# A Mamba block and a table-coded FFN on one core: the time steps move in the merged stages, three pieces of work move in the prologue

## The chip, the cores and the metric

One core of a Trainium2 chip runs the whole kernel in one launch. The time is the device time of that core in microseconds (us). The engines, by the names of the profile: PE is TensorE, DVE is VectorE, ACT is ScalarE, POOL is GpSimd, SP is SyncE, which here only issues DMAs. Each engine works through its own queue in order; they wait for each other on semaphores.

## The reference

For an input of 4 x 1024 tokens of 512 numbers:

```python
x = x + layernorm(mamba(layernorm(x)))          # mamba: below
x = x + layernorm(ffn(layernorm(x)))
# mamba(u): proj = u @ W_in.T, split into z (512), x (512), B (64), C (64), dt (8 heads)
#   x, B, C = silu(causal_conv4(x, B, C));  dt = softplus(dt + dt_bias);  dA = exp(-exp(A_log) * dt)
#   S = S * dA_t + dt_t * outer(x_t, B_t);  y_t = S @ C_t          (a scan over the tokens of a sequence)
#   y = (y + D * x) * silu(z);  return y @ W_out.T
# ffn(x): w = lut[idx] for the three matrices (16 values), h = silu(x @ gate.T) * (x @ up.T), h @ down.T
```

`W_in` is 1160 x 512, the FFN's inner width is 1376. State and `dt` are per head (8 heads of 64).

## The kernel before

**Tiles and stages.** The 4096 tokens are cut into 8 tiles of 512 tokens (t = 0 to 7), each of 4 chunks of 128. Every fp32 operand of a large product is split into two fp16 halves, so that a product is three matmuls. After a prologue the kernel runs 8 stages and two tails. Stage t does the scan of tile t chunk by chunk (four phases: `scan(t, c)` on PE, `y_sum`, `y_gated`, `y_split` on DVE, `segments`, `weights`, `decay_state` on POOL) and prepares tile t+1: its projections, the causal convolution of five blocks of 128 channels (`conv`, order 4, 0, 1, 2, 3, block 4 being B and C), the gates `z`, and the time steps. In stages 0 and 1 (`dec`) the FFN's weights are decoded beside this: ACT turns codes into fp16 (`codes_to_half`), DVE makes eight masks for each unit of 832 columns (`masks`), PE multiplies them with a diagonal of the table's values (`decode`), ACT copies the result (`decoded`). In stages 2 to 7 (`ffn`, "merged stages") the FFN of tile g = t - 2 runs beside the scan: `gate_up(g, m)` for 11 blocks m, then `down(g, c)` for 4 chunks. The two tails are the FFN of tiles 6 and 7.

**What sets the order.** Every engine's order of work is written out by hand in its own `stage(t)` function (POOL L670, ACT L910, PE L1346, DVE L1694, SP's L465 and L509), and its prologue ahead of them. Nothing is planned at run time: an instruction whose input is late holds up all behind it on its engine.

**PE and its banks.** `gate_up(g, m)` (L1312) writes gate m, then up m, into three PSUM banks in turn. Turn n needs the bank of turn n - 3 read: gate m is read by `gate_silu(g, m)`, up m by `times_up(g, m)`, both DVE, and both count on the semaphore `ffn_turn`. So up 7 (turn 15) needs `gate_silu(6)` and what stands before it in DVE's queue, gate 8 needs `times_up(6)`, up 8 needs `gate_silu(7)`, up 9 needs `gate_silu(8)`. In the second phase of a merged stage PE does: scan 1, projections of dt and conv 4, gate/up 5, `prepare` and segment sums of chunk 2, gate/up 6, conv 0, gate/up 7, `project_out` 1, gate/up 8; then scan 2, conv 1, gate/up 9.

**DVE's second phase** in `stage` (L1745 to L1791): y of chunk 1, `dt_input(t+1)`, `conv(t+1, 4)`, `gate_silu(5)`, `times_up(5)`, `weigh`, `decayed`, `conv_silu(t+1, 4)`, `time_steps(t+1)`, `ln_stats("x", t-1, 0)`, `gate_silu(6)`, `low(5)`, `times_up(6)`, `conv(t+1, 0)`, `gate_silu(7)`, `low(6)`, `conv_silu(t+1, 0)`, `times_up(7)`, `gate_silu(8)`, `low(7)`, `times_up(8)`; then `y_sum(t, 2)`.
`time_steps(i)` (L1562) is a chain of 18 instructions on 128 x 32 numbers: the softplus's series, `da` in two fp16 halves (step 20 of `dt_steps`), and `dt4` (step 21). Its readers are `segments(t+1, 0)` on POOL (L597), which waits for step 20, PE's `prepare_small(t+1, 0)` and POOL's `weights(t+1, 0)`, all in the fourth phase. `ln_stats` (L1517) takes mean and variance of a pair of slices (two `bn_stats`, two `bn_aggr`); POOL's `pair_rstd` (L585, five small operations) makes the scale and shift of them; ACT's `normalise_slice` (L775) applies them. POOL's `pair_rstd("x", t-1, 0)` stands between `weights(t, 2)` and `decay_state(t, 2)`.

**The prologue.** Input slices 0 are normalised, transposed and projected; `W_in` is scaled and split on ACT and DVE (`high_half`, `low_half`); the same is done for `W_out`, whose scale (`scales(1)` and `c_out`) DVE makes after a maximum over partitions on POOL (L758). ACT's `high_half(3)` (L1132) waits for it on `s_wscale`, and DVE's `out_weights_low` in stage 0 needs that. DVE's order from L1974: `dt_input(0)`, out scale, `conv(0, 0)`, `conv_silu(0, 4)`, `conv_silu(0, 0)`, `time_steps(0)`, `conv(0, 1)`, `ln_stats("u", 1, 0)`, `z_gate(0, 0)`, `conv(0, 2)`, `conv_silu(0, 1)`, `conv(0, 3)`, `conv_silu(0, 2)`, `clear_state(0)`, `z_gate(0, 1)`, `conv_silu(0, 3)`, `weigh(0, 0)`, `decayed(0, 0)` (the first decayed gram), `z_gate(0, 2)`, `masks(0)`, `z_gate(0, 3)`. On POOL, `pair_rstd("u", 1, 0)` (L764) stands ahead of `segments(0, 0)` and `weights(0, 0)`. On ACT `codes_to_half(3)` (L1151) waits until all of `masks(0)` is made.

Of the kernel before, what the change touches and what calls it, by code (L numbers as in the profile page):

```python
# [120 lines left out]
def sandwich_kernel(nc, u, w_in_t, conv_w, conv_b, w_out_t, a_log, d_param, dt_bias, lut, codes, out):  # L121
# [31 lines left out]
    with ctx:  # L153
# [242 lines left out]
        with nc.Block() as block:  # L396
# [184 lines left out]
            def _(pool):  # L581
# [3 lines left out]
                def pair_rstd(kind, tile, b):  # L585
                    no = pair_no[kind, tile, b]
                    i = no % 2
                    v = vare[:, i, :]
                    pool.wait_ge(ln_steps.sem, ln_steps.now(no, 4))
                    for n, (dst, a, b, op) in enumerate((  # L590
                            (v, mv[:, i, :, 1], eps_c[:, 0:2], ALU.add), (v, v, neg_half[:, 0:2], ALU.pow),
                            (rstd[:, i, :], v, xs_c[:, 0:2], ALU.mult), (v, mv[:, i, :, 0], neg_one[:, 0:2], ALU.mult),
                            (shift[:, i, :], v, rstd[:, i, :], ALU.mult))):
                        rstd_steps.inc(nc.gpsimd.tensor_tensor(dst, a, b, op))  # L594
                        pool.wait_ge(rstd_steps.sem, rstd_steps.now(no, n + 1))

                def segments(t, c):  # L597
                    if t > 0 or c > 0:
                        pool.wait_ge(y_done.sem, y_done.now(t, c))
                    if c == 0:  # L600
                        pool.wait_ge(dt_steps.sem, dt_steps.now(t, 20))
                    for n in range(2):
                        seg_ready.inc(nc.gpsimd.tensor_tensor(  # L603
                            segs[:, n], causal_h[:].unsqueeze(1).broadcast_to((P, HEADS, P)),
                            da[:, t % HALVES, c, n, :].unsqueeze(2).broadcast_to((P, HEADS, P)), ALU.mult))
# [64 lines left out]
                def stage(t):  # L670
                    g = t - LAG
                    nxt = t + 1 < TILES

                    decay_state(t, 0)
                    segments(t, 1)
                    if t >= 1:
                        out_rstd(t - 1, 3)
                        add_residual(t - 1, 3)
                    weights(t, 1)
                    if nxt:  # L680
                        pair_rstd("u", t + 1, 1)

                    decay_state(t, 1)
                    segments(t, 2)
                    out_rstd(t, 0)
                    add_residual(t, 0)
                    weights(t, 2)
                    if t >= 1:
                        pair_rstd("x", t - 1, 0)

                    decay_state(t, 2)
                    segments(t, 3)
                    out_rstd(t, 1)
                    add_residual(t, 1)
                    weights(t, 3)

                    decay_state(t, 3)
                    if nxt:
                        segments(t + 1, 0)
                    if g >= 0:  # L700
                        down_rstd(g, 0)
                    out_rstd(t, 2)
                    if g >= 0:
                        add_output(g, 0)
                    add_residual(t, 2)
                    if g >= 0:
                        down_rstd(g, 1)
                    if nxt:
                        weights(t + 1, 0)
                    if t >= 1:  # L710
                        pair_rstd("x", t - 1, 1)
                    if g >= 0:
                        add_output(g, 1)
                        down_rstd(g, 2)
                        add_output(g, 2)
                    if t + 2 < TILES:
                        pair_rstd("u", t + 2, 0)
                    if g >= 0:
                        down_rstd(g, 3)
                        add_output(g, 3)  # L720

                def tail(t):
# [38 lines left out]
                    diag[:], fold[:].unsqueeze(1).unsqueeze(1).broadcast_to((P, PAIRS, 2, NST)),  # L761
                    lut_sel[:].rearrange("p n q -> p q n").unsqueeze(3).broadcast_to((P, PAIRS, 2, NST)),
                    ALU.mult).then_inc(s_diag, 1)
                pair_rstd("u", 1, 0)  # L764
                segments(0, 0)
                weights(0, 0)
                for t in range(TILES):
# [5 lines left out]
            def _(act):  # L773
# [71 lines left out]
                def codes_to_half(k):  # L845

                    if k >= HALF_UNITS:
                        return
                    act.wait_ge(s_codes[k % 2], 32 * (k // 2 + 1))
                    if k >= CODE_SLOTS:  # L850
                        act.wait_ge(s_masks, 2 * (k - CODE_SLOTS + 1))
                    nc.scalar.activation(codes_h[:, k % CODE_SLOTS, :], codes_sb[:, k % 2, :], ACT.Identity,
                                         bias=pair_bias[:]).then_inc(s_half, 1)
# [248 lines left out]
                def high_half(n):  # L1102
                    src, hi, _, which = PIECES[n]
                    act.wait_ge(s_wscale if which else s_scale, 1)
                    nc.scalar.activation(hi, src, ACT.Copy, scale=wscale[:, which:which + 1]).then_inc(s_whi if which else s_hi, 1)
# [23 lines left out]
                conv_input(0, 0)  # L1129
                dt_exponential(0)  # L1130
                conv_tanh(0, 4)
                high_half(3)  # L1132
                conv_tanh(0, 0)
                conv_input(0, 1)
                act.wait_ge(s_pair, 1)
# [12 lines left out]
                codes_to_half(1)  # L1148
                z_tanh(0, 3)
                codes_to_half(2)  # L1150
                codes_to_half(3)  # L1151
                for t in range(TILES):
                    stage(t)
# [334 lines left out]
            def _(dve):  # L1488
# [51 lines left out]
                def conv_silu(i, f):  # L1540
                    o = CONV_ORDER.index(f)
                    half = i % HALVES
                    dve.wait_ge(ctanh_ready.sem, ctanh_ready.now(i, o + 1))
                    if f < KC:
                        xs_ready.inc(nc.vector.scalar_tensor_tensor(
                            xs[:, half, f, :], conv_in(i, o)[:, 0:TILE], 1.0, xs[:, half, f, :], ALU.add, ALU.mult))
                    else:
                        h = slice(half * NST, (half + 1) * NST)
                        for dst, lo in ((bs, 0), (cs, NST)):
                            xs_ready.inc(nc.vector.scalar_tensor_tensor(  # L1550
                                dst[h, :], cin[lo:lo + NST, o % 2, 0:TILE], 1.0, conv_sum(i, f)[lo:lo + NST, :],
                                ALU.add, ALU.mult))
# [101 lines left out]
                def gate_silu(g, m):  # L1654
                    w = MW[m]
                    dve.wait_ge(gtanh_ready.sem, gtanh_ready.now(g, m + 1))
                    ffn_turn.inc(nc.vector.scalar_tensor_tensor(  # L1657
                        gact[0:w, :], gact[0:w, :], 1.0, banks[FFN_BANKS[2 * m % 3]][0:w, :], ALU.add, ALU.mult))
# [35 lines left out]
                def stage(t):  # L1694
# [69 lines left out]
                    decayed(t, 2)  # L1764
                    if nxt:
                        conv_silu(t + 1, 4)
                        time_steps(t + 1)
                    if ffn_next:
                        ln_stats("x", t - 1, 0)
                    if ffn:  # L1770
                        gate_silu(g, 6)
# [10 lines left out]
                        conv_silu(t + 1, 0)  # L1782
                    if ffn:
                        times_up(g, 7)
                        gate_silu(g, 8)
                        low(g, 7)
                        times_up(g, 8)
# [131 lines left out]
                def scales(k):  # L1919
# [5 lines left out]
                    step(nc.vector.reciprocal(wscale[:, one], expo[:, one]))  # L1925
                    step(nc.vector.tensor_scalar(wscale[:, one], wscale[:, one], WS, None, ALU.mult))

                def out_weights_low():
                    low_half(3)
                    step(nc.vector.tensor_scalar(c_gate_half[:], expo[:, 2:3], 0.5 / (XS * WS), None, ALU.mult))  # L1930
                    step(nc.vector.tensor_scalar(c_down[:], expo[:, 2:3], expo[:, 2:3], 32.0 / WS, ALU.mult, ALU.mult))
                    step(nc.vector.tensor_scalar(c_down[:], c_down[:], expo[:, 2:3], None, ALU.mult))
# [7 lines left out]
                dve.wait_ge(s_lut, 16)  # L1940
                step(nc.vector.tensor_reduce(big[:, 2:3], lut_sb[:], AX_X, ALU.max, apply_absolute_value=True))
                scales(2)
                ln_stats("u", 0, 0)
                ln_stats("u", 0, 1)

# [20 lines left out]
                for n in range(3):  # L1966
# [5 lines left out]
                step(nc.vector.tensor_scalar(a_sb[:], a_sb[:], -SEG, None, ALU.mult))  # L1972
                conv(0, 4)
                dt_input(0)  # L1974
                dve.wait_ge(s_wall, 1)
                scales(1)
                nc.vector.tensor_scalar(c_out[:], c_in[:], expo[:, 1:2], 0.25 / (WS * WS), ALU.mult,
                                        ALU.mult).then_inc(s_wscale, 1)
                conv(0, 0)
                conv_silu(0, 4)  # L1980
                conv_silu(0, 0)
                time_steps(0)
                conv(0, 1)
                ln_stats("u", 1, 0)
                z_gate(0, 0)
                conv(0, 2)
                conv_silu(0, 1)
                conv(0, 3)
                conv_silu(0, 2)
                clear_state(0)  # L1990
                z_gate(0, 1)
                conv_silu(0, 3)
                weigh(0, 0)
                decayed(0, 0)
                z_gate(0, 2)
                masks(0)
                z_gate(0, 3)
                for t in range(TILES):
# [42 lines left out]
```

## Time and profile before

| | us |
|---|---|
| median of 3 runs (all: 1426.32, 1434.93, 1438.0) | 1434.93 |
| the profiled execution, its own time | 1433.22 |
| its span, first to last instruction | 1431.1 |
| mean granted clock of PE over the span | 0.963 |

All further numbers of the profile come from that one execution; the time and the span differ by 2.1 us that lie around the instructions. The granted clock is 1.00 at 2.4 GHz and 0.50 at 1.2 GHz. "Idle before" is the time in which an engine stood still ahead of an instruction, with what ended it. On POOL, spans are rough.

### The profile page before, as it was taken

The page shows a single profiled execution, that of the slowest core. Times are in us where ns is not written, and L with a number is a line of the kernel's source. Part 1 is how long each engine was busy: PE and PEld are TensorE (multiplying, and loading weights), DVE is VectorE, ACT ScalarE, POOL GpSimd, SP SyncE. Part 2 cuts the span into 40 slices and gives each one's busy share as a digit, 9 for nine tenths or more (in the row PEclk, how much of TensorE's full clock was granted, in tenths as well). Part 3 has the DMA queues.
Part 4 walks back from the last instruction along what each step waited for, and adds up shares of the span by engine and source line. Part 5 has one row for each costly group of instructions (what it writes and reads, how often), then busy time and mean ns, then how long its engine had stood idle before and what let it go on. Part 6 is the DMA issues. An engine that isn't in the chain of part 4 may idle for free. (4 is left out here: it accounts for less than half of the span.)

```text
span 1431.1 us, 18648 instructions
## 1 busy us (share of the span) xinstructions
PE 1323.5 (92%) x6656; PEld 636.8 (44%) x6656; DVE 964.0 (67%) x1895; ACT 547.0 (38%) x986; POOL 521.2 (36%) x723
## 2 busy tenths in 40 slices
PE   4759988988899999999999999999999999999998
PEld 2324434434444444454444444444444444444443
DVE  7977776887668766876687667765777466543432
ACT  5465565656443424342434224333333232122120
POOL 1413334432333453335433543453533444310102
PEclk9888889979999999999999999999999999999999
DMA  5143323521331233123311422123212211411201
GB/s 165 36 104 85 82 70 101 137 63 59 67 81 23 60 102 82 22 46 110 73 39 30 109 76 52 30 70 93 74 27 50 72 50 40 108 41 30 74 0 52
DMA packets 132812, 96.16 MB, mean 67 GB/s; under 512 B 102000, under 2 KB 102000, under 8 KB 132720
## 3 DMA queue, kind: packets, MB, share of 16 engines
q1 hardware_dynamic: 130832, 94.94, 25.4%
q8 instruction: 53, 0.87, 0.2%
q10 hardware_dynamic: 1888, 0.03, 0.1%
q14 instruction: 39, 0.32, 0.1%
HBM read 54.05 MB, written 16.78 MB: 49 GB/s over the span
## 5 line engine op out<-in xcount | busy, mean ns | idle before, releaser
L1328 PE MATMUL bank<-fxt,ffn_hi 128*128 128x512 f16 (+1 forms) x1408 | 422.8, 382 | 17.3 <-DVE gact L1657 15.4
L1328 PE MATMUL bank<-fxt,ffn_lo 128*128 128x512 f16 (+1 forms) x704 | 268.7, 382 | 0.0
L1328 PEld LDWEIGHTS bank<-fxt,ffn_hi 128*128 128x128 f16 (+1 forms) x1408 | 139.8, 101 | 190.9 <-DVE gact L1657 20.8
L1234 PE MATMUL bank<-mask,diag 128*128 128x416 f16 x640 | 140.0, 375 | 54.4 <-ACT ffn_lo L863 41.5
L638 POOL TENSOR_TENSOR state<-state,ex 64x512 f32<-64x512 f32 x32 | 35.5, 1108 | 329.2 <-PE bank L1291 328.2
L1342 PE MATMUL bank<-ffn_hi,h_hi 128*128 128x512 f16 (+1 forms) x352 | 133.5, 379 | 0.0
L1342 PE MATMUL bank<-ffn_hi,h_lo 128*128 128x512 f16 (+1 forms) x352 | 133.4, 379 | 0.0
L1342 PE MATMUL bank<-ffn_lo,h_hi 128*128 128x512 f16 (+1 forms) x352 | 133.3, 379 | 0.0
L603 POOL TENSOR_TENSOR decay<-causal_h,da 128x1024 f16<-128x1024 f16 x64 | 120.9, 1911 | 28.6 <-PE bank L1295 23.0
L1657 DVE SCALAR_TENSOR_TENSOR gact<-gact,bank 128x512 f32<-128x512 f32 (+1 forms) x88 | 60.2, 684 | 104.0 <-ACT gact L902 103.3
L1234 PEld LDWEIGHTS bank<-mask,diag 128*128 128x128 f16 x640 | 64.5, 105 | 131.9 <-ACT ffn_lo L863 48.2
L1508 DVE TENSOR_SCALAR mask<-codes_h 128x832 f16<-128x832 f16 x320 | 112.5, 410 | 8.2 <-PE bank L1234 7.8
L1536 DVE SCALAR_TENSOR_TENSOR xs<-cin,conv_w_sb,xs 128x512 f32<-128x512 f32 x114 | 106.9, 937 | 15.4 <-ACT xs L817 12.3
L902 ACT ACTIVATE gact<-bank,c_gate_half 128x512 f32<-128x512 f32 (+1 forms) x88 | 59.9, 681 | 144.8 <-PE bank L1328 143.0
L1328 PEld LDWEIGHTS bank<-fxt,ffn_lo 128*128 128x128 f16 (+1 forms) x704 | 70.9, 101 | 82.8 <-issue 2.4
L1202 PE MATMUL bank<-xt,win_hi 128*128 128x512 f16 x320 | 97.0, 385 | 4.1 <-DVE win_lo L1916 4.1
L908 ACT ACTIVATE h_hi<-hf 128x512 f16<-128x512 f32 (+1 forms) x88 | 55.1, 626 | 100.4 <-DVE hf L1666 100.0
L1172 PE MATMUL bank<-win_hi,xt 128*128 128x512 f16 (+1 forms) x512 | 92.1, 275 | 0.0
L780 ACT ACTIVATE ut<-ut,shift,rstd 128x512 f32<-128x512 f32 x62 | 49.8, 804 | 90.6 <-POOL shift L594 90.6
L1172 PE MATMUL bank<-wout_hi,yt 128*128 128x512 f16 x256 | 82.4, 383 | 0.0
L1666 DVE SCALAR_TENSOR_TENSOR hf<-gact,bank 128x512 f32<-128x512 f32 (+1 forms) x88 | 60.4, 686 | 31.7 <-PE bank L1328 25.3
L1530 DVE TENSOR_TENSOR xsplit<-ut,xsplit 128x512 f16<-128x512 f32 x62 | 42.9, 699 | 55.0 <-ACT xsplit L788 54.7
(186 smaller groups left out, 2202.5 us busy)
## 6 DMA issues: line engine op xcount, KB each, us to landing
codes_sb<-codes SPq DMA_DIRECT2D x80, 208.0 KB, 3.4
ures<-u SPq DMA_DIRECT2D x32, 256.0 KB, 2.9
x_scratch<-x SPq DMA_DIRECT2D x32, 256.0 KB, 2.4
ut<-x_scratch SPq DMA_DIRECT2D x16, 512.0 KB, 4.4
xres<-x_scratch SPq DMA_DIRECT2D x32, 256.0 KB, 3.1
out<-dn SPq DMA_DIRECT2D x32, 256.0 KB, 2.0
ut<-u SPq DMA_DIRECT2D x15, 512.0 KB, 4.4
ffn_hi<-w_in_t SPq DMA_DIRECT2D x4, 580.0 KB, 8.7
```

The lines of the kernel that those rows point to most:

```text
L603: seg_ready.inc(nc.gpsimd.tensor_tensor(segs[:, n], causal_h[:].unsqueeze(1).broadcast_to((P, HEADS, P)), da[:, t % HALVES, c, n, :].unsqu ...
L902: gtanh_ready.inc(nc.scalar.activation(gact[0:w, :], banks[FFN_BANKS[2 * m % 3]][0:w, :], ACT.Tanh, scale=c_gate_half[0:w, :]))
L908: hhi_ready.inc(nc.scalar.activation(h_hi[0:w, m, :], hf[0:w, :], ACT.Copy))
L1172: last = nc.tensor.matmul(out_ap, lhs, rhs, start=(k == 0), stop=(k == len(pairs) - 1))
L1202: last = nc.tensor.matmul(p.bank[:], w[:, k, cols], xt[:, :, half, k, :], start=(k == 0 and n == 0), stop=(k == KC - 1 and n == 2))
L1234: last = nc.tensor.matmul(p.bank[:, 0:COLS], diag[:, q].rearrange("p n m -> p (n m)"), mask[:, n, q, j * COLS:(j + 1) * COLS], start=(q == ...
L1328: last = nc.tensor.matmul(bank, wt[:, c0:c0 + w], fxt[:, :, half, k, :], start=(k == 0 and n == 0), stop=(k == KC - 1 and n == 2))
L1342: last = nc.tensor.matmul(banks[FFN_BANKS[turn % 3]][:], h[0:w, m, tok], wt[0:w, d0:d0 + D], start=(m == 0 and n == 0), stop=(m == MB - 1 ...
L1508: ins = nc.vector.tensor_scalar(mask[:, n, q, :], codes_h[:, count % CODE_SLOTS, :], float(2 * q), None, ALU.is_equal)
L1536: chain(conv_steps, i, CSTEPS * o + k, nc.vector.scalar_tensor_tensor(conv_sum(i, f), conv_in(i, o)[:, k:k + TILE], conv_w_sb[:, f, k:k + ...
L1657: ffn_turn.inc(nc.vector.scalar_tensor_tensor(gact[0:w, :], gact[0:w, :], 1.0, banks[FFN_BANKS[2 * m % 3]][0:w, :], ALU.add, ALU.mult))
L1666: ffn_turn.inc(nc.vector.scalar_tensor_tensor(hf[0:w, :], gact[0:w, :], HSCALE, banks[FFN_BANKS[(2 * m + 1) % 3]][0:w, :], ALU.mult, ALU.m ...
```

## The change

1. DVE, `stage`: in the merged stages `time_steps(t+1)` and `ln_stats("x", t-1, 0)` move from ahead of `gate_silu(g, 6)` to behind `times_up(g, 7)`, now in the order `ln_stats`, `time_steps`. In stages 0 and 1 both stay. In stage 7, which prepares no tile, only `ln_stats` moves.
2. DVE, prologue: the first tile's `clear_state(0)` moves up, ahead of the first `ln_stats`; the out weights' scale becomes a function `out_scale` and moves behind `decayed(0, 0)`; `ln_stats("u", 1, 0)` moves behind `z_gate(0, 2)`.
3. POOL: `pair_rstd("u", 1, 0)` moves from ahead of `segments(0, 0)` into stage 0, behind `segments(0, 1)`.
4. ACT: `high_half(3)` moves from ahead of `conv_tanh(0, 0)` to between `codes_to_half(2)` and `codes_to_half(3)`.

```diff
@@ POOL stage
                     segments(t, 1)
+                    if t == 0:
+                        pair_rstd("u", 1, 0)
@@ POOL prologue
-                pair_rstd("u", 1, 0)
                 segments(0, 0)
@@ ACT prologue
                 conv_tanh(0, 4)
-                high_half(3)
                 conv_tanh(0, 0)
...
                 codes_to_half(2)
+                high_half(3)
                 codes_to_half(3)
@@ DVE stage
                     if nxt:
                         conv_silu(t + 1, 4)
+                    if dec:
                         time_steps(t + 1)
-                    if ffn_next:
+                    if dec and ffn_next:
                         ln_stats("x", t - 1, 0)
...
                     if ffn:
                         times_up(g, 7)
+                        ln_stats("x", t - 1, 0)
+                    if ffn and nxt:
+                        time_steps(t + 1)
+                    if ffn:
                         gate_silu(g, 8)
@@ DVE prologue
+                def out_scale():
+                    dve.wait_ge(s_wall, 1)
+                    scales(1)
+                    nc.vector.tensor_scalar(c_out[:], c_in[:], expo[:, 1:2], 0.25 / (WS * WS), ALU.mult,
+                                            ALU.mult).then_inc(s_wscale, 1)
...
                 scales(2)
+                clear_state(0)
                 ln_stats("u", 0, 0)
...
                 dt_input(0)
-                dve.wait_ge(s_wall, 1)
-                scales(1)
-                nc.vector.tensor_scalar(c_out[:], c_in[:], expo[:, 1:2], 0.25 / (WS * WS), ALU.mult,
-                                        ALU.mult).then_inc(s_wscale, 1)
                 conv(0, 0)
...
                 conv(0, 1)
-                ln_stats("u", 1, 0)
                 z_gate(0, 0)
...
                 conv_silu(0, 2)
-                clear_state(0)
                 z_gate(0, 1)
...
                 decayed(0, 0)
+                out_scale()
                 z_gate(0, 2)
+                ln_stats("u", 1, 0)
                 masks(0)
```

## Rows read from the trace of the kernel before

**Rows 1.** The page, busy us (share of the span) x instructions, each engine
```profile
PE 1323.5 (92%) x6656; PEld 636.8 (44%) x6656; DVE 964.0 (67%) x1895; ACT 547.0 (38%) x986; POOL 521.2 (36%) x723
```

**Rows 2.** Waits of PE, longest in total first: us, times, longest
```profile
PE bank L1234 <- ACT ffn_lo L863: 41.5, 14, 6.8
PE bank L1328 <- DVE gact L1657: 15.4, 11, 2.2
...
PE bank L1234 <- DVE mask L1508: 12.9, 9, 3.5
PE bank L1278 <- POOL decay L603: 7.5, 1, 7.5
```

**Rows 3.** Timeline of PE: start, us, instruction, [idle before it <- releaser]
```profile
410.90 0.60 PE L1328 MATMUL bank<-fxt,ffn_hi 128*128 128x512 f16 x2 [0.91 <-DVE gact L1657]
...
449.04 0.60 PE L1328 MATMUL bank<-fxt,ffn_hi 128*128 128x512 f16 x2 [2.15 <-DVE gact L1657]
...
1044.91 0.61 PE L1328 MATMUL bank<-fxt,ffn_hi 128*128 128x512 f16 x2 [2.08 <-DVE gact L1657]
```

**Rows 4.** Windows, PE on line L1328: length, busy (x), granted clock, DMA, GB/s
```profile
597.00:601.00 4.00, 2.76 (x12) 1.00 0.00 0
745.30:748.70 3.40, 3.40 (x9) 0.51 0.00 0
...
1045.70:1049.10 3.40, 3.40 (x10) 0.50 0.00 0
```

**Rows 5.** Timeline of DVE in the second phase of stage 6
```profile
1038.62 0.18 DVE L1565 TENSOR_SCALAR dtp<-dte 128x32 f32<-128x32 f32 x1
...
1042.58 0.18 DVE L1582 TENSOR_SCALAR dt<-dt 128x32 f32<-128x32 f32 x1
...
...
1044.20 0.66 DVE L1657 SCALAR_TENSOR_TENSOR gact<-gact,bank 128x512 f32<-128x512 f32 x1
...
1055.30 0.69 DVE L1657 SCALAR_TENSOR_TENSOR gact<-gact,bank 128x512 f32<-128x512 f32 x1 [4.26 <-ACT gact L902]
...
1060.57 0.69 DVE L1615 TENSOR_TENSOR y<-y,bank 128x512 f32<-128x512 f32 x1 [1.66 <-PE bank L1295]
```

**Rows 6.** Timeline of POOL, same phase: the decay of the state
```profile
1058.41 1.03 POOL L638 TENSOR_TENSOR state<-state,ex 64x512 f32<-64x512 f32 x1 [12.25 <-PE bank L1291]
```

**Rows 7.** Timeline of DVE in the prologue
```profile
44.67 2.32 DVE L1536 SCALAR_TENSOR_TENSOR xs<-cin,conv_w_sb,xs 128x512 f32<-128x512 f32 x3
47.02 1.29 DVE L1522 BATCH_NORM_STATS2 stats<-ut 128x6 f32<-128x512 f32 x2
...
52.09 5.47 DVE L1536 SCALAR_TENSOR_TENSOR xs<-xsplit,conv_w_sb,xs 128x512 f32<-128x512 f32 x3
...
58.33 0.48 DVE L1652 MEMSET state<- 64x512 f32 x1
...
59.84 0.69 DVE L1545 SCALAR_TENSOR_TENSOR xs<-xsplit,xs 128x512 f32<-128x512 f32 x1 [0.48 <-ACT xsplit L825]
...
62.51 7.45 DVE L1508 TENSOR_SCALAR mask<-codes_h 128x832 f16<-128x832 f16 x8
```

**Rows 8.** Timelines of POOL, PE and ACT in the prologue
```profile
51.58 4.64 POOL L603 TENSOR_TENSOR decay<-causal_h,da 128x1024 f16<-128x1024 f16 x2
62.51 1.26 POOL L612 TENSOR_TENSOR xdt<-xtok,dt 128x512 f32<-128x512 f32 x1 [6.29 <-ACT xtok L872]
...
67.81 3.89 POOL L603 TENSOR_TENSOR decay<-causal_h,da 128x1024 f16<-128x1024 f16 x2
...
56.28 1.89 PE L1278 MATMUL bank<-decay,below_h 128*128 128x512 f16 x4 [7.50 <-POOL decay L603]
...
34.80 1.99 ACT L1105 ACTIVATE wout_hi<-ffn_hi,wscale 128x2048 f16<-128x2048 f32 x1
```

**Rows 9.** Instructions of line L1632 (ns min/median/max, first and last start)
```profile
L1632 DVE TENSOR_SCALAR ymax<-ymax x32: 140/153/155, 77.2 to 1232.0; 128x1 f32<-128x1 f32 x32
```

**Rows 10.** Windows, PE: length, busy (x), granted clock, DMA share, GB/s
```profile
0.00:400.00 400.00, 316.81 (x1617) 0.88 0.32 87
```

## The prediction

> **What bounds the kernel now.** I read the page's busy times first, then the list of TensorE's waits, then the idle pieces of its timeline, and the granted clock beside them. TensorE is busy 92% of the span, VectorE 67% [rows 1], so only time in which TensorE stands still, or runs at its lower clock, is to be had. Its waits [rows 2] fall into two parts. The waits of the decoding matmuls (L1234: 41.5 us on ScalarE's copies and 12.9 us on VectorE's masks) and the 7.5 us before the first segment sums belong to the prologue and stages 0 and 1, the first 400 us. The 15.4 us in 11 pieces "L1328 <- DVE gact L1657" belong to the merged stages, where TensorE is otherwise without a gap. The timeline shows these 11 as a pair in each of the stages t = 2 to 6, some 0.92 us (first at 410.90) and then 1.96 to 2.15 us (449.04, 597.10, 745.29, 895.04, 1044.91), and one of 0.54 us in the tail [rows 3]. The five longer ones sum to 15.4 - 5 x 0.92 - 0.54 = 10.3 us. The clock has more to tell: behind the gaps at 745, 895 and 1045 the granted clock is 0.50 for 3.4 us (1.2 GHz instead of 2.4; the first and the last of the three are shown), behind those at 449 and 597 it stays at 1.00 [rows 4].
>
> **The merged stages: what the longer gap is.** VectorE's timeline around 1044.91 says it [rows 5]. `time_steps(7)` begins at 1038.62, its last instruction ends at 1042.76, `ln_stats("x", 5, 0)` follows, and only at 1044.20 does `gate_silu(g, 6)` start, which ends at 1044.86. TensorE had finished gate 7 at 1042.83; up 7 takes the third bank in turn and needs `gate_silu(6)` to have read it, so it starts at 1044.91. The tanh that `gate_silu(6)` needs was there before 1038.62 (no idle time stands ahead of it): it is queued behind 1044.20 - 1038.62 = 5.58 us of work that nobody waits for yet.
>
> **The change there** puts both calls behind `times_up(g, 7)`. Nothing is added or removed: 18 small instructions and 4 of statistics per stage, no DMA. Then `gate_silu(6)` starts at about 1038.6 and ends at 1039.3, 3.5 us before TensorE wants the bank. What is late next? I follow the queue on. `low(5)` and `times_up(6)` run to 1040.7; `conv(t+1, 0)` waits for ScalarE's first tap (there by 1042) and ends at 1044.3; `gate_silu(7)`, `low(6)`, `conv_silu(0)`, `times_up(7)` take it to 1046.8; the two moved calls 5.6 us more, to 1052.4. `gate_silu(8)` would have its tanh at about 1051.3, since TensorE is now 2.1 us ahead: it becomes 1.1 us late. In the old order VectorE sat idle 4.26 us just there [rows 5], which is the cover that takes the move. Who waits for `gate_silu(8)`? Up 9, behind scan 2, the conv projection and gate 9, some 9 us later: not reached. `y_sum(t, 2)` starts up to 1 us later than it could, but its second addition now waits 1.66 us for TensorE [rows 5], which covers it. On GpSimd, `pair_rstd("x")` stands ahead of `decay_state(t, 2)`; the old order leaves 12.25 us between them [rows 6], the new one 12.25 - 4.1 - 2.1 = 6 us. The time steps themselves are first used by `segments(t+1, 0)` behind scan 3, a whole phase on. So the gap goes entirely: bounds 0 (something unseen takes its place) and 10.3 us; I take 10.3, because every next user has microseconds to spare. Stage 7 has no time steps and no gap; moving its `ln_stats` costs nothing, TensorE being covered there.
>
> The clock: three of the five gaps were followed by 3.4 us at half rate, in which TensorE did half its work, 3 x 1.7 = 5.1 us. After none of the 0.92 us gaps did it fall. With the 2 us gap gone I expect no fall: bounds 0 and 5.1 us, and 5.1 us taken, since the fall begins within 0.8 us of the gap's end all three times.
>
> **The prologue.** The headline is that TensorE idles 7.5 us until 56.28 because `segments(0, 0)` on GpSimd starts only at 51.58 [rows 8], behind `pair_rstd("u", 1, 0)`, itself behind VectorE's `ln_stats("u", 1, 0)` at 47.02 [rows 7]. With `pair_rstd` behind `segments(0, 1)`, the segments start when the time steps are there, at 44.6: 7 us earlier. That is not 7 us of gain, for the end of the prologue is VectorE's. From 34.5 to 70 us it idles 0.48 us in all [rows 7], and every instruction that the change takes out of the way (`out_scale`, `ln_stats`) comes back ahead of `masks(0)`. Two things shape the sum.
> First, GpSimd and VectorE block each other: the three taps of `conv(0, 3)` took 5.47 us beside `segments(0, 0)`, where `conv(0, 1)` alone took 2.32 [rows 7]. Now it is `conv(0, 1)` that meets the segments: +3.15 there, -3.15 later, nil.
> Second, the saved pieces: the state's memset (0.48 us) goes into VectorE's wait for the first slices, and the 0.48 us wait at 59.84 should go because ScalarE has `decays(0, 0)` done by then. Step by step: `conv(0, 1)` ends at 50.1, `z_gate` 50.7, `conv(0, 2)` 53.1, `conv(0, 3)` 56.0, `conv_silu(0, 3)` 58.0 (before: 60.5), `decayed(0, 0)` 59.5, `out_scale` (five steps of 0.15 [rows 9] and the gaps between them) 60.5, `z_gate` 61.1, `ln_stats` 62.7, `masks(0)` from 62.7, as before from 62.51. There GpSimd's `weights(0, 0)` started 3 us earlier, but its two long segment operations are still ahead, and I let the masks through at one or two for each GpSimd operation: end near 69.8, before 69.96 [rows 7]. Gain 0.1 to 0.5. Bounds: from -2.8 (below) to +3 (the whole lead of `conv_silu(0, 3)` kept); I take 0.5.
> `high_half(3)` (1.99 us on ScalarE [rows 8]) moves into the wait of `codes_to_half(3)` for `masks(0)`; it has `out_scale` since 60.5 and is done by 64, and `out_weights_low` wants it after 80. It queues nothing but that conversion. `pair_rstd("u", 1, 0)`, five small operations, falls behind the segments that ended at 71.7 [rows 8], where GpSimd next waits for the tokens of chunk 1, which ScalarE copies behind `decoded(0, 0)` and `codes_to_half(5)`, and ScalarE's `normalise_slice` of that pair is queued behind `decays(0, 1)`. Both cost nothing; if the cover went, 2 us each, once.
> One rule of the Trainium skill speaks against `out_scale` in its new place: its page SBUF — State Buffer (Who interferes with whom) says that `tensor_scalar` can run in a mode that takes the port pair shared with GpSimd, and that the later of two such instructions blocks entirely. By it alone each of the steps may wait for one GpSimd operation. The trace's nearest row is the same form on one column in `y_split`: 140 to 155 ns in all 32 [rows 9], never stretched, though no row proves that GpSimd ran beside every one.
>
> **Sum**, against the profiled execution's own 1433.2 us: 1433.2 - 10.3 - 5.1 - 0.5 = 1417.3. The median of the runs shown is 1434.9, 1.7 above it, and they spread over 12 us; I put the median after at 1418.
>
> **The rivals.**
> A. The clock does not come back: two of the five gaps had no fall behind them, so the three falls may have another cause, or new falls come elsewhere. Only 10.8 us: about 1423. 20%.
> B. A new wait takes the gap's place in each merged stage. The time steps now sit ahead of `gate_silu(8)` beside `pair_rstd`, and their two-input steps can wait for its operations; were VectorE as late there as TensorE was idle, half of the gap would return: 5 x 1 us, with clock falls rarer: about 1427. For it: VectorE's lateness at `gate_silu(8)` of 1.1 us or more; against it: the 9 us before anyone needs it. 10%.
> C. The prologue loses. `out_scale`'s five steps meet the operations of `weights(0, 0)`, of 1.26 us each [rows 8]; three of them wait for one, less the 0.15 that each takes itself: 3 x 1.1 = 3.3 us later for `ln_stats` and `masks(0)`, against 0.5 gained: -2.8, and 1433.2 - 15.4 + 2.8 = about 1421. 8%. (The Trainium skill's rule above gives this time.)
> D. Slower than before. The idle of the first stages is only rearranged, and TensorE's lower clock spreads in them. Over the first 400 us the mean granted clock is 0.88 [rows 10], so some 2 x 0.12 x 400 = 96 us were at half rate, and TensorE is busy 317 of the 400. Each further microsecond at half costs up to 0.79 / 2 = 0.4 us. It outweighs the 15.4 us of the merged stages from 39 us more at half; with 60 us more it is 24 us, about 1442. For it: the mix of short gaps and half clock there is fragile, and the runs' spread is likely from it. Against it: the order of the decoding itself is untouched. 3%.
> E. The forecast, 59%; own range 1412 to 1423.
>
> **How the numbers follow.** About 1% (14.3 us, below 1420.6) is what a measurement of this kernel tells from no change. Four fifths of E lie below that (0.47), and a third of A to C by the spread of the early stages (0.08, less 0.02 for the run-to-run medians): faster 0.53, within 1% 0.44, slower 0.03. The range takes in A, C and most of B: 1410 to 1428.
>
> **What would show it.** In the profile after: "L1328 <- DVE gact" down from 15.4 to some 5 us in 6 pieces of 0.92 and less; the stages 4 to 6 no longer at 149.8 us from gap to gap but near 146.1; granted clock 1.00 from 400 us on; VectorE's idle time before `gate_silu(8)` gone; the memset at 5 us; the segments at 44.6 us and the wait before the first segment sums under 1 us; `masks(0)` starting within 1 us of 62.5. I am wrong about the mechanism if a gap of over 1 us stands anywhere in stages 2 to 6, and about the prologue if scan 0's `y_sum` starts more than 2 us from 70.5.

## The result and the profile after

| | before | after |
|---|---|---|
| median, us (4 runs each) | 1436.15 | 1416.39 |
| lowest to highest | 1426.32 to 1438.0 | 1412.15 to 1418.8 |
| profiled execution, us | 1433.22 | 1412.15 |
| its span | 1431.1 | 1410.1 |

The ratio is 0.9875, with a 95% interval from 0.983 to 0.992: faster, by about 1.2%. In a second comparison (below), of 6 runs with 11, it is 0.9896 (0.9874 to 0.9917). The medians are 19.8 us apart here and 15.0 us there; the second rests on more runs. 1418 us were forecast. One of the six runs of `merged_only` (below) took 2709.39 us, nearly twice the others, at a granted clock of 1.00; no trace of it was kept, its cause is open, and all figures below leave it out.

The profiled execution after is the fastest of its four, 4 us under the median, so the difference of the two spans (21.0 us) is more than the change is worth. Where it comes from shows in the waits of PE in the kernel after (us in total, times, longest); they answer to [rows 2]:

```profile
PE bank L1235 <- ACT ffn_lo L864: 46.3, 14, 6.9
...
PE bank L1235 <- DVE mask L1509: 14.0, 9, 3.5
PE bank L1329 <- DVE gact L1658: 5.1, 6, 0.9
PE bank L1254 <- DVE xs L1546: 4.4, 1, 4.4
...
PE bank L1173 <- DVE zs L1588: 1.0, 1, 1.0
```

The line numbers are one higher where the new lines of code stand above. "L1329 <- DVE gact" was 15.4 us in 11 pieces and is 5.1 in 6: the five long ones are gone, the five of 0.92 us and the one in the tail are as they were. The wait for the segment sums (7.5 us) is gone from the list, but 5.4 us stand in its place: PE now waits for a `z_gate` and for the last `conv_silu` of the prologue. The two short waits for GpSimd that stood there (`xdt` 1.0 us, `xtok` 0.6 us) are gone too. The decoding's waits (41.5 and 12.9 before) are not smaller.

The two pieces in the timeline of PE, kernel after, that answer to [rows 3] (first and fourth of the merged stages; nothing stands between them but the like ones at 552.32 and 698.25):

```profile
406.40 0.61 PE L1329 MATMUL bank<-fxt,ffn_hi 128*128 128x512 f16 x2 [0.92 <-DVE gact L1658]
...
844.17 0.61 PE L1329 MATMUL bank<-fxt,ffn_hi 128*128 128x512 f16 x2 [0.92 <-DVE gact L1658]
```

A stage lasts (844.17 - 406.40) / 3 = 145.92 us from gap to gap; before it was 148.25, 148.06, 149.9 and 149.8. The clock, in the windows of PE (length, busy and number, granted clock, DMA share, GB/s), kernel after:

```profile
0.00:400.00 400.00, 314.65 (x1646) 0.90 0.34 89
400.00:1400.00 1000.00, 993.18 (x4999) 1.00 0.23 60
```

It no longer falls anywhere between 400 and 1400 us.

VectorE in the second phase of stage 6, kernel after, timeline; it answers to [rows 5]:

```profile
1021.17 0.69 DVE L1551 SCALAR_TENSOR_TENSOR cs<-cin,xs 64x512 f32<-64x512 f32 x1
1021.89 0.69 DVE L1658 SCALAR_TENSOR_TENSOR gact<-gact,bank 128x512 f32<-128x512 f32 x1
...
1029.43 0.68 DVE L1667 SCALAR_TENSOR_TENSOR hf<-gact,bank 128x512 f32<-128x512 f32 x1
1030.03 1.28 DVE L1523 BATCH_NORM_STATS2 stats<-ut 128x6 f32<-128x512 f32 x2
1031.23 0.41 DVE L1526 BATCH_NORM_AGGREGATE mv<-stats 128x2 f32<-128x6 f32 x2
1031.55 0.15 DVE L1566 TENSOR_SCALAR dtp<-dte 128x32 f32<-128x32 f32 x1
...
1035.62 0.68 DVE L1658 SCALAR_TENSOR_TENSOR gact<-gact,bank 128x512 f32<-128x512 f32 x1
...
1039.54 0.69 DVE L1616 TENSOR_TENSOR y<-y,bank 128x512 f32<-128x512 f32 x1 [1.21 <-PE bank L1296]
```

`gate_silu(6)` runs right behind `conv_silu(4)` now. The statistics and the time steps stand from 1030.03 to 1035.62 (5.59 us, as before), and `gate_silu(8)` follows without idle time, where VectorE had 4.26 us of it. The second addition of `y_sum` still waits 1.21 us for PE (1.66 before): what the new order makes late is absorbed there.

A measure free of the early stages is the time from stage 2's 0.92 us gap to the end of the span: 1431.1 - 410.90 = 1020.2 before, 1410.1 - 406.40 = 1003.7 after. So 16.5 of the 21.0 us are the merged stages' and 4.5 lie ahead of 410 us.

### The profile page after: what moved, and what is told of

Read it like the earlier page. It is cut to its first block and busy times, and to the rows that moved or that the text cites. A ratio compares the mean times of both kernels' runs of the same rounds, so it can differ in the third digit from the quotient of the medians.

```text
span 1410.1 us, 18646 instructions
## 1 busy us (share of the span) xinstructions
PE 1310.8 (93%) x6656; PEld 633.1 (45%) x6656; DVE 964.8 (68%) x1895; ACT 547.3 (39%) x986; POOL 522.0 (37%) x723
## 5 line engine op out<-in xcount | busy, mean ns | idle before, releaser
L1329 PE MATMUL bank<-fxt,ffn_hi 128*128 128x512 f16 (+1 forms) x1408 | 419.0, 379 | 6.8 <-DVE gact L1658 5.1
L1329 PE MATMUL bank<-fxt,ffn_lo 128*128 128x512 f16 (+1 forms) x704 | 266.8, 379 | 0.0
L1329 PEld LDWEIGHTS bank<-fxt,ffn_hi 128*128 128x128 f16 (+1 forms) x1408 | 139.4, 100 | 177.0 <-DVE gact L1658 8.1
L1329 PEld LDWEIGHTS bank<-fxt,ffn_lo 128*128 128x128 f16 (+1 forms) x704 | 70.4, 100 | 81.5
L594 POOL TENSOR_TENSOR vare<-mv,eps_c 128x2 f32<-128x2 f32 x32 | 17.3, 541 | 176.1 <-DVE mv L1526 176.0
```

What stands on the lines that cost most here:

```text
L1329: last = nc.tensor.matmul(bank, wt[:, c0:c0 + w], fxt[:, :, half, k, :], start=(k == 0 and n == 0), stop=(k == KC - 1 and n == 2))
```

## The experiments

All were compared with runs of the kernel before on the same chip. Their median was 1431.43 us (17 runs) for the first four experiments, and 1431.25 us (11 runs) for `gap_longer`, `rstd_late`, `both_gaps` and `after_again`.

**One part alone, first the merged stages.** The edit is that of DVE's `stage` in the change, on the kernel before.

> Only the merged stages' part: time_steps and ln_stats(x) behind times_up(7); the prologue as before. My theory (the 2 us gap and the fall of the clock behind it are most of the gain): PE's waits on gact fall from 15.4 to 5.1 us, the stages from gap to gap last 145.9 us, the clock is 1.00 from 400 us on; ratio 0.989 to 0.990 (14 to 16 us less), the first gap of stage 2 stays within 3 us of 410.9. Rival (the prologue and the first stages carry a good part): not more than 11 us less, ratio 0.992 or above.

Measured: 1415.86 us (median of the five runs that count), 15.6 us less; ratio 0.9908 (0.989 to 0.9927), which is 13.2 us. In its profile (span 1411.1) the wait for gact is 5.1 us in 6 pieces, the gaps stand at 407.31, 553.22, 699.13, 845.04 and 990.96, 145.91 apart, and the clock is 1.00 from 400 to 1400 us. From the gap of stage 2 to the end: 1003.8 us. By the medians the gain is inside the 14 to 16 us expected, by the ratio just short of it; either is nearly the whole of the change's gain. The interval of the ratio still touches the rival's 0.992. What speaks against the rival is the stretch behind the gap of stage 2, 16.4 us shorter than before, and the next experiment.

**The prologue alone.** The edits of POOL, ACT and of DVE's prologue, with the merged stages as before.

> Only the prologue's part (clear_state, out_scale, ln_stats(u,1,0), pair_rstd, high_half moved); the merged stages as before. My theory: scan 0's y_sum starts at 68.9 instead of 70.5, 1.5 us earlier, and the rest of the early stages differs only by where the clock happens to fall, so the median is 1 to 2 us less, ratio 0.998 to 1.000, not told from 1. Rival: the 3 us more that the changed kernel had gained by 406 us are also the prologue's: 4.5 us less, ratio 0.997.

Measured: 1430.5 us (12 runs), ratio 0.9994 (0.998 to 1.0009): not told from no change. The first `y_sum` starts at 68.75 us, as expected. But the 70.47 of the kernel before, with which that was to be compared, is not fixed. Nine profiles have either the old prologue or the new one, whatever their merged stages (us; the last column is the first instruction of `y_split(0, 0)`, which multiplies y by the gate):

| | first convolution | `masks(0)`: start, length | first `y_sum` | `y_split(0, 0)` |
|---|---|---|---|---|
| old: before | 30.56 | 62.51, 7.45 | 70.47 | 75.38 |
| old: merged_only | 30.23 | 62.17, 7.45 | 70.14 | 75.05 |
| old: stats_only | 30.75 | 62.57, 7.47 | 70.56 | 75.48 |
| old: steps_only | 29.53 | 61.34, 4.06 | 65.92 | 74.03 |
| old: gap_longer | 29.87 | 61.70, 2.37 | 65.13 | 74.91 |
| new: after | 30.07 | 61.65, 6.77 | 68.94 | 73.85 |
| new: after_again | 30.31 | 61.90, 7.22 | 69.64 | 74.55 |
| new: both_gaps | 30.05 | 61.63, 6.76 | 68.90 | 73.81 |
| new: prologue_only | 29.82 | 61.47, 6.76 | 68.75 | 73.66 |

With the old prologue `masks(0)` took 7.45 to 7.47 us where GpSimd's `weights(0, 0)` began with it or at most 0.3 us behind it, and 4.06 or 2.37 us where VectorE was the first by 1.2 and 1.4 us; the first `y_sum` then started 2.8 us or more before that of any new prologue. Timelines of VectorE and GpSimd, `steps_only`, then `gap_longer`:

```profile
61.34 4.06 DVE L1508 TENSOR_SCALAR mask<-codes_h 128x832 f16<-128x832 f16 x8
62.58 1.17 POOL L612 TENSOR_TENSOR xdt<-xtok,dt 128x512 f32<-128x512 f32 x1 [7.52 <-ACT xtok L872]
```

```profile
61.70 2.37 DVE L1508 TENSOR_SCALAR mask<-codes_h 128x832 f16<-128x832 f16 x8
63.12 1.85 POOL L612 TENSOR_TENSOR xdt<-xtok,dt 128x512 f32<-128x512 f32 x1 [7.70 <-ACT xtok L872]
```

In these two the masks after `y_sum` take 5.19 us instead of 2.36, so most of the lead is lost again by `y_split(0, 0)`. Counted from the first convolution, `y_split(0, 0)` comes after 44.50 to 45.04 us with the old prologue and after 43.76 to 44.24 with the new: about 0.9 us is what the nine profiles support, and not 1.5. Nothing of it can be made out at the gap of stage 2, at 407.31 to 412.91 with the old prologue and at 406.40 to 413.81 with the new.

The 3 us more that the changed kernel had by 406 us are not the prologue's either: in this profile the first 0.92 us gap comes at 413.81, later than before. A further execution of the changed kernel shows the same. Timeline of PE, the changed kernel run again:

```profile
413.66 0.60 PE L1329 MATMUL bank<-fxt,ffn_hi 128*128 128x512 f16 x2 [0.91 <-DVE gact L1658]
```

The same program reached this point at 406.40 in one execution and at 413.66 in another, and these took 1412.15 and 1419.62 us: nearly the whole difference is in the first 400 us. Beyond this gap the two agree within 0.2 us (1003.7 and 1003.9). The granted clock of the first 400 us was 0.90 in the one and 0.88 in the other.

**Which of the two calls makes the gap.** `stats_only` moves `ln_stats("x")` alone:

```diff
-                    if ffn_next:
+                    if dec and ffn_next:
                         ln_stats("x", t - 1, 0)
...
                         times_up(g, 7)
+                        ln_stats("x", t - 1, 0)
                         gate_silu(g, 8)
```

> Only ln_stats(x) moves behind times_up(7) in the merged stages; time_steps stays ahead of gate_silu(6). The gap before up 7 is 2.08 less the 1.53 of the statistics, 0.5 to 0.6 us in each of five stages. If the fall of the clock hangs on the length of the gap, it does not fall in the merged stages (as it never did behind the 0.92 us gaps): 7.7 + up to 5.1 us less, ratio 0.991 to 0.994. Rival (the falls have another cause): up to three falls of 3.4 us stay behind the shortened gaps.

`steps_only` moves the other one alone:

```diff
                         conv_silu(t + 1, 4)
+                    if dec:
                         time_steps(t + 1)
...
                         times_up(g, 7)
+                    if ffn and nxt:
+                        time_steps(t + 1)
+                    if ffn:
                         gate_silu(g, 8)
```

> Only time_steps moves behind times_up(7); ln_stats(x) stays ahead of gate_silu(6). gate_silu(6) then ends some 1.5 us after conv_silu(4), 2 us before PE wants the bank: the gap is gone just as with both moved, so ln_stats need not have moved. 14 to 16 us less, same as merged_only within 2 us. Rival (both are needed): a gap of over 0.3 us stays before up 7.

Measured: `stats_only` 1422.14 us, ratio 0.9938 (0.9917 to 0.9958), 9.3 us less; `steps_only` 1417.1 us, ratio 0.9903 (0.9887 to 0.9919), 14.3 us less. PE in `stats_only`: its wait list, then its last gap before up 7 in the timeline, then its window from 400 us:

```profile
PE bank L1328 <- DVE gact L1657: 7.7, 11, 0.9
```

```profile
1033.89 0.61 PE L1328 MATMUL bank<-fxt,ffn_hi 128*128 128x512 f16 x2 [0.56 <-DVE gact L1657]
```

```profile
400.00:1300.00 900.00, 891.75 (x4534) 1.00 0.25 63
```

As expected: of the 5.58 us ahead of `gate_silu(6)`, taking 1.5 away leaves gaps of 0.44 to 0.58 us, and the clock stays up behind all five. Taking the time steps away leaves none (5.1 us in 6 pieces, 1003.8 us from the gap of stage 2 to the end, as with both moved). So the move of `ln_stats` was not needed, and did no harm.

**Does the clock fall because of the gap?** In stages 2 to 6 of the kernel before, ahead of `gate_silu(g, 6)`:

```diff
+                    if ffn and nxt:
+                        for _ in range(11):
+                            step(nc.vector.tensor_scalar(dtp[:], dt[:], 0.25, None, ALU.mult))
                     if ffn:
                         gate_silu(g, 6)
```

> The kernel before, with 11 more small instructions (0.25 x dt into a scratch, some 2.1 us, their result is read by nobody) behind time_steps and ln_stats in stages 2 to 6, so that the gap before up 7 is 4.1 to 4.3 us instead of 2.1. My theory (a fall of the clock follows the gap and is the likelier the longer the gap is): the clock falls behind all five, at some 741 to 1055 us and also behind the first two; 10.5 us more for the gaps and 1.7 us or more for each fall that the kernel before lacks: 14 to 22 us more. Rival (the falls have nothing to do with the gap): 10.5 us more, and as few falls as before.

Measured: 1451.8 us, ratio 1.014 (1.0114 to 1.0166), 20.5 us more. Two of the five gaps in the timeline of PE, and the windows where its clock was low (length, busy, granted clock, DMA, GB/s):

```profile
453.39 0.61 PE L1328 MATMUL bank<-fxt,ffn_hi 128*128 128x512 f16 x2 [4.49 <-DVE gact L1657]
...
1063.86 0.61 PE L1328 MATMUL bank<-fxt,ffn_hi 128*128 128x512 f16 x1 [4.48 <-DVE gact L1657]
```

```profile
453.90:457.30 3.40, 3.40 (x10) 0.51 0.00 0
604.00:610.80 6.80, 5.28 (x13) 0.50 0.00 0
757.60:764.40 6.80, 5.68 (x14) 0.50 0.00 0
911.20:914.60 3.40, 2.61 (x7) 0.51 0.00 0
1061.40:1068.20 6.80, 4.34 (x11) 0.50 0.00 0
```

All five gaps now come with a fall, three of them twice as long as any that the kernel before had from 400 us to the last 4 us. The gaps were 4.36 to 4.49 us, a little over the 4.1 to 4.3 expected. The part of the time that belongs to the clock: 1450.7 - 412.91 = 1037.8 us from the gap of stage 2 to the end, 34.0 more than without any gap (1003.8); 27.2 - 5.1 = 22.1 us of that are the gaps, the rest, 11.9, is mostly the clock: half of the 21.31 us in which PE worked at half rate is 10.7. Three of the five falls begin before the gap has ended (at 604.0, 757.6 and 1061.4). The rival (falls have nothing to do with the gap) is refuted.

**Is the 7.5 us wait of the prologue worth anything?** The kernel before with `pair_rstd("u", 1, 0)` moved alone:

```diff
-                pair_rstd("u", 1, 0)
                 segments(0, 0)
...
                     segments(t, 1)
+                    if t == 0:
+                        pair_rstd("u", 1, 0)
```

> The kernel before with pair_rstd(u, 1, 0) alone moved behind segments(0, 1), so that segments(0, 0) start when the time steps are there. The 7.5 us wait of PE before the first segment sums should shrink to under 1 us. My theory (VectorE's queue sets the end of the prologue, and the collision with GpSimd only moves from conv(0, 3) to conv(0, 1)): the first y_sum starts within 1 us of 70.5 all the same. Rival (that wait is worth what it shows): y_sum starts 4 us or more earlier, at 66.5 or before.

Measured: one run, 1431.42 us. The wait for the segment sums is gone, but 6.0 us of it come back. PE's wait list, and VectorE's timeline:

```profile
PE bank L1254 <- DVE xs L1546: 3.5, 1, 3.5
PE bank L1173 <- DVE zs L1588: 2.5, 1, 2.5
```

```profile
44.21 5.48 DVE L1537 SCALAR_TENSOR_TENSOR xs<-cin,conv_w_sb,xs 128x512 f32<-128x512 f32 x3
...
61.49 9.11 DVE L1509 TENSOR_SCALAR mask<-codes_h 128x832 f16<-128x832 f16 x8
...
71.12 0.68 DVE L1611 TENSOR_TENSOR y<-bank,ex 128x512 f32<-128x512 f32 x1
```

The collision moved from `conv(0, 3)` to `conv(0, 1)` at the same price (5.48 us for three taps; [rows 7] have 5.47 and, without it, 2.32). `masks(0)` starts 1 us earlier than before and takes 9.11 us instead of 7.45: two of its eight masks now take 2.06 us each beside GpSimd's two long segment operations, where in the kernel before it was one. The first `y_sum` starts at 71.12 and `y_split(0, 0)` at 76.03, both later than in any of the nine profiles above. So the wait was a symptom; VectorE's queue, with its collisions, set the end. This rests on a single profile, and on a distance to the rival's 66.5 us that the old prologue itself covers in two of five.

**The other gap.** The 0.92 us gap that was left has the same form: in stages 2 to 6 `ln_stats("u", t+1, 1)` waits for a load while `decayed(t, 1)` and `gate_silu(2)` are queued behind it. On the changed kernel:

```diff
-                    if ffn and nxt:
-                        ln_stats("u", t + 1, 1)
                     decayed(t, 1)
...
                         gate_silu(g, 2)
                         low(g, 1)
                         times_up(g, 2)
+                    if ffn and nxt:
+                        ln_stats("u", t + 1, 1)
```

> The changed kernel with one more move in the merged stages: ln_stats(u, t+1, 1), which stands behind weigh(t, 1) and waits there for a load (VectorE idle 4.23 us before it at 1003 us), goes behind times_up(g, 2). Then decayed(t, 1) and gate_silu(2) are no longer queued behind that load, and the 0.92 us gap before gate/up 3 should go in five stages: 4.6 us less than the changed kernel, stages of 145.0 us; ratio 0.986 to 0.987 against the kernel before. Rival (gate_silu(2) is late for another reason, or pair_rstd(u, t+1, 1) on GpSimd, late by 3 us, holds up decay_state(t, 1)): no less than the changed kernel, or the gap moves to another place.

The changed kernel ran beside it:

> The changed kernel itself, beside the same runs of the kernel before as the others of this call. If the two parts add (0.9908 for the merged stages, 0.9994 for the prologue), the ratio is 0.990, 14 us less; rival (together they give more than apart, as the first comparison's 0.9875 may say): 0.988 or below.

Measured: `after_again` 1416.23 us, ratio 0.9896 (0.9874 to 0.9917); `both_gaps` 1409.9 us, ratio 0.9848 (0.9824 to 0.9872), 21.4 us less than before and 6.3 less than the changed kernel. The parts of the change add up (0.9908 and 0.9994 make 0.990); the first comparison's 0.9875 is not told from that. In `both_gaps` PE's timeline has no gap between the decoding and the tails; what is left of its waits past 400 us, and its window there:

```profile
PE bank L1329 <- DVE dn L1692: 1.4, 2, 1.2
...
PE bank L1329 <- DVE gact L1658: 0.5, 1, 0.5
PE bank L1329 <- DMA fxt<-xsplit: 0.3, 1, 0.3
```

```profile
400.00:1400.00 1000.00, 997.71 (x5024) 1.00 0.24 61
```

PE is busy 997.7 of 1000 us there (993.2 in the changed kernel): 4.5 us, the five gaps of 0.92. The rest of the median's 6.3 us is not accounted for; the wandering of the early stages is enough for it. `pair_rstd` of that pair ran at 987.79, 12 us before `decay_state(t, 1)` at 999.50. This version beats both kernels.

## Why the prediction was right

**What the longer gap is, and that it goes entirely** (10.3 us taken of bounds 0 and 10.3): right. All five gaps are gone, `merged_only` shows it without the rest, and `steps_only` and `stats_only` show that 5.58 us of queued work were the cause, the 4.1 us of the time steps alone being enough. What would be late next was followed through the queue, and came as worked out: the idle time before `gate_silu(8)` gone, `y_sum` covered by its wait for PE, `pair_rstd` finished at 1033.6 ahead of a `decay_state` at 1037.73, 4.2 us of slack where 6 were reckoned.

**The clock** (5.1 us for three falls): right in kind, too large in size for a usual execution. Between the two profiled executions it came as worked out: 16.5 us from stage 2's gap to the end against 10.3 + 5.1 = 15.4. Of the 1.1 us over, some 0.9 is that each removed gap took 0.17 us or so more than its length (148.25 - 145.92 = 2.33 for one of 2.15); what that is made of no run shows. But how many of the five gaps are followed by a fall changes from execution to execution. It was three in the kernel before, one in `prologue_only` and one in `rstd_late`, each with five such gaps. Windows of PE, `prologue_only`, then `rstd_late`:

```profile
1044.20:1047.60 3.40, 3.40 (x9) 0.50 0.00 0
```

```profile
747.70:751.10 3.40, 3.40 (x9) 0.50 0.00 0
```

The prediction took the three falls of its one profile as fixed. By the three profiles together it is 1.7 falls, or 2.8 us, and 10.3 + 0.9 + 2.8 = 14.0 us is an estimate that fits `steps_only` (14.3) and `merged_only` (13.2 to 15.6). Rival A (the falls have another cause) is refuted by the longer gap.

**The prologue** (0.5 us, bounds -2.8 to +3): inside the bounds, and the measured effect on the time (0.9994, or 0.9 us, interval from 2.9 less to 1.3 more) is told neither from 0.5 nor from nothing. The step that was off is the start and the length of `masks(0)`: the working had it from 62.7 to 69.8, it ran from 61.65 to 68.4. Part of the earlier start is no gain: the first convolution began 0.5 us earlier, which is within its wandering (29.53 to 30.75 with the old prologue). And the length that the working leaned on, 7.45 us, is one of several that the old prologue takes (see the table above). The timeline of VectorE and that of GpSimd, kernel after:

```profile
57.50 1.22 DVE L1598 TENSOR_TENSOR decay<-decay,gram 128x1024 f32<-128x1024 f32 x1
58.65 0.15 DVE L1928 TENSOR_SCALAR big<-big 128x1 f32<-128x1 f32 x1
...
59.21 0.15 DVE L1932 TENSOR_SCALAR wscale<-wscale 128x1 f32<-128x1 f32 x1
...
60.13 1.28 DVE L1523 BATCH_NORM_STATS2 stats<-ut 128x6 f32<-128x512 f32 x2
...
61.65 6.77 DVE L1509 TENSOR_SCALAR mask<-codes_h 128x832 f16<-128x832 f16 x8
68.34 0.68 DVE L1588 SCALAR_TENSOR_TENSOR zs<-zs,bank 128x512 f32<-128x512 f32 x1
68.94 0.68 DVE L1611 TENSOR_TENSOR y<-bank,ex 128x512 f32<-128x512 f32 x1
```

```profile
58.69 1.04 POOL L612 TENSOR_TENSOR xdt<-xtok,dt 128x512 f32<-128x512 f32 x1 [10.60 <-ACT xtok L873]
59.69 1.05 POOL L616 TENSOR_TENSOR xd<-xtok,d_sb 128x512 f32<-128x512 f32 x1
60.91 1.04 POOL L623 TENSOR_TENSOR xtok<-xdt,ex 128x512 f32<-128x512 f32 x1 [0.17 <-POOL xd L616]
```

The out weights' scale, the `z_gate` and the statistics ran beside `weights(0, 0)` and neither side was slowed: one-column steps of 0.15 us, GpSimd's operations of 1.04 us, which took 1.26 beside the masks [rows 8]. So work that does not collide took the masks' place beside GpSimd. That this is where the 0.9 us come from is likely, but no run takes the three moves apart. It also answers rival C: no step of `out_scale` waited. The broad reading of the Trainium skill's page SBUF — State Buffer (Who interferes with whom) that `tensor_scalar` contends does not hold for one column; the page itself makes it hang on the operands' conditions, and the trace decides for this form.
That the wait before the segment sums would be worth nearly nothing was right as far as the one profile of `rstd_late` goes. What the prediction left unsaid is where PE would wait instead (5.4 us at the `z_gate` and the transposes of chunk 0).

**Rival B** (a new wait in the merged stages): no trace of it. **Rival D** (slower): the early stages do wander, by 7 us between two executions of one program, but around nearly the same middle with the old and the new prologue (means of 410.8 and 411.3 us at the gap of stage 2, five and three profiles).

**The sum**: 1418 us against 1416.4 and 1416.2 measured. Some of that closeness is luck. The forecast stood 16.9 us under a median of three runs, 1434.9, which the larger sets put at 1431.4 and 1431.25; measured were 19.8 us less in the first comparison and 15.0 in the second. Of the terms, 10.3 came as 11.2 with what each gap costs beyond its length, 5.1 was what three falls cost and is nearer to 2.8 for a usual execution, and 0.5 was nearer to 0.9; the errors offset each other. In the chances, a third of the 0.38 of A to C is 0.13 and not 0.08, which would have made "faster" 0.58. Rival B's 1427 us takes back the clock's 5.1 us as well as half of the gaps, while its words have the falls rarer.

## What to carry to other kernels

Where the engine that bounds a kernel stands still behind another's instruction, look at what is queued ahead of that instruction and at when its results are first read: here 4.1 us of small steps, read a phase later, stood ahead of a bank's release, and moving them into idle time of their own engine gave 1%. A long wait need not be worth its length: in the one profile that tried it, the 7.5 us of the prologue were worth nothing alone, since another engine's queue ended the stretch, while 2 us gaps cost more than their length through the clock. Two ways of telling chance from effect helped: the part alone, and the time from a landmark of the trace to the end, which left out the first stages' 7 us of wandering. A landmark serves only if it holds still: the first `y_sum` moved by 5 us between executions of the same prologue, so a gain of 1.5 us read from one pair of profiles meant little.

## What the runs showed of the hardware

TensorE's granted clock fell to 1.2 GHz at 5 of 15 gaps of 1.93 to 2.15 us (three profiles: 3, 1 and 1), at all 5 gaps of 4.36 to 4.49 us, and at none of the 50 gaps of 0.44 to 0.93 us in the merged stages of nine profiles; around each of them TensorE was otherwise busy without a break. A fall at a 2 us gap lasted 3.4 us, those at the 4.4 us gaps 3.4 or 6.8, and three of these began inside the gap. That a third of the 2 us gaps is hit and the others are not can make some of the spread from run to run, about 1.7 us for each fall (149.75 us with one and 148.06 without, for two stages of the kernel before with a gap of 1.96 us each). I had not expected that gaps of one length go both ways.

VectorE's masks (fp16, 128 x 832) and GpSimd's operations slowed each other by an amount that hung on which began first: eight masks took 2.37 us where GpSimd's first operation began 1.4 us behind them (it took 1.85 us then, against 1.04 us beside `out_scale`), 4.06 us where it began 1.2 us behind them, and 6.76 to 7.47 us in the seven profiles in which GpSimd was already at work or began within 0.3 us.
